# Expert entries: the hidden tile split into fp16 parts first and turned by a transposing DMA, with the down product one entry later

## The reference

```python
x = x + xattn(layernorm(x), ctx_512, Wq, Wkv_expand, Wout)      # 8 x 512 tokens of 512, 16 heads, 64 keys
x = x + ffn(layernorm(x), router_w, wg, wu, wd, sg_*, su_*, sd_*)

def ffn(x):
    logits = x @ router_w.T
    scores, top_idx = top_k(logits, 2)                          # 2 of 8 experts for each token
    comb = zeros((T, 8)).at[arange(T)[:, None], top_idx].set(scores)
    h = silu(x @ wg[e]) * (x @ wu[e])                           # 256 wide, for each expert e
    y = h @ wd[e]
    return sum_e(y * comb[:, e]) + shared_expert(x)
```

## Time and profile before

| | |
|---|---|
| median of 3 executions | 908.63 us |
| the profiled execution's own time | 908.0 us |
| its span, first to last instruction | 905.8 us |
| PE busy | 814.4 us (90%) |
| weight loads | 549.3 us (61%) |
| DVE busy | 664.5 us (73%) |
| ACT busy | 406.4 us (45%) |
| POOL busy | 379.6 us (42%) |
| DMA queue of SP (q1) | 29.5% of 16 engines |
| DMA queue of POOL (q0) | 22.3% of 16 engines |

### The profile page before, as it was taken

How to read it: one execution, slowest core, us unless ns; L and a number is a source line. 1 busy time by engine, 2 the same in 40 slices (tenths; PEclk the granted TensorE clock), 3 DMA queues, 4 the chain that set the end, 5 groups by cost and what they waited for, 6 DMA issues and landing times.

```text
span 905.8 us, 22405 instructions
## 1 busy us (share of the span) xinstructions
PE 814.4 (90%) x7626; PEld 549.3 (61%) x7626; DVE 664.5 (73%) x1352; ACT 406.4 (45%) x737; POOL 379.6 (42%) x486
## 2 busy tenths in 40 slices
PE   5378999888888888898999789999999999999995
PEld 2267777767666777676787668555555555555552
DVE  4999999999999999986467888555555555555552
ACT  3355757575657666666432223333333333333331
POOL 1114545454545364544300001355555655555553
PEclk9789999999999999999999999999999999999998
DMA  8233453536363634244675456375656666666661
GB/s 313 94 87 139 123 173 114 198 94 205 105 205 105 183 116 125 84 117 147 215 230 176 141 162 202 96 122 104 117 107 117 116 108 115 112 111 117 112 111 16
DMA packets 64136, 123.08 MB, mean 136 GB/s; under 512 B 15744, under 2 KB 16768, under 8 KB 62656
## 3 DMA queue, kind: packets, MB, share of 16 engines
q1 hardware_dynamic: 48160, 86.43, 29.5%
q0 software_dynamic: 15904, 35.70, 22.3%
HBM read 71.61 MB, written 52.31 MB: 137 GB/s over the span
## 4 chain that ended last, share of the span: by engine, by line
PE 49%; DVE 29%; issue 11%; POOL 5%; ACT 3%; DMA 1%; DVEq 1%; POOLq 1%; SPq 0%; ACTq 0%
PE psum L1202 34%; PE psum L1250 8%; PE psum L1193 6%; DVE stats L863 4%; DVE head_max L939 3%; DVE probsT L788 3%; DVE xy L949 2%; POOL kv_store L526 2%; DVE xn1T L788 2%; DVE emag L875 1%; DVE qT L788 1%; POOL rstd L507 1%; DVE probs L935 1%; DVE attnT L914 1%; DVE emax L890 1%
## 5 line engine op out<-in xcount | busy, mean ns | idle before, releaser
L616 POOL DMA_INDIRECT x_in<-normed_tokens,tabs x71 | 70.4, 991 | 228.8 <-DVE y_w L1150 126.5
L626 POOL DMA_INDIRECT out<-w_q,tabs x71 | 112.5, 1585 | 43.5 <-issue 18.1
L1168 DVE SCALAR_TENSOR_TENSOR hid<-psum,tabs,silu_g 128x256 f32<-128x256 f32 x71 | 34.3, 484 | 111.8 <-ACT silu_g L750 111.8
L1202 PE MATMUL psum<-exp_all,hidT 128*128 x426 | 103.5, 379 | 1.0 <-DVE hidT L1136 1.0
L1250 PE MATMUL psum<-xn1T,w_q 128*128 128x128 f16 x1536 | 93.5, 222 | 7.1 <-DVE xn1T L788 7.0
L750 ACT ACTIVATE silu_g<-psum,tabs 128x256 f32<-128x256 f32 x71 | 33.7, 474 | 146.1 <-PE psum L1202 146.1
L1202 PE MATMUL psum<-exp_all,probsT 128*128 x420 | 96.4, 379 | 0.0
L1250 PEld LDWEIGHTS psum<-xn1T,w_q 128*128 128x128 f16 x1536 | 88.5, 99 | 8.1 <-DVE xn1T L788 7.8
L1202 PE MATMUL psum<-w_o,attnT 128*128 128x512 f16 x384 | 89.0, 382 | 0.0
L505 POOL TENSOR_SCALAR rstd<-moments 128x1 f32<-128x1 f32 x64 | 14.2, 223 | 171.1 <-DVE moments L866 167.3
L518 POOL TENSOR_TENSOR exp_all<-piece,exp_all 128x512 f32 (+1 forms) x48 | 56.0, 1166 | 45.5 <-ACT piece L646 45.5
(11 more groups left out here) (197 smaller groups left out, 1704.8 us busy)
## 6 DMA issues: line engine op xcount, KB each, us to landing
x_in<-x SPq DMA_DIRECT2D x64, 256.0 KB, 3.0
exp_all<-experts SPq DMA_DIRECT2D x8, 1536.0 KB, 7.2
out<-xy SPq DMA_DIRECT2D x32, 256.0 KB, 2.0
normed_tokens<-xn SPq DMA_DIRECT2D x32, 256.0 KB, 2.1
normed_turned<-xn2T SPq DMA_DIRECT2D x32, 256.0 KB, 2.0
w_q<-out SPq DMA_DIRECT2D x32, 256.0 KB, 3.0
out<-w_q SPq DMA_DIRECT2D x32, 256.0 KB, 2.2
probsT<-normed_turned SPq DMA_DIRECT2D x16, 256.0 KB, 4.1
```

Source lines behind the costliest of these rows:

```text
L616: pool.indirect_dma_start(x_in[:, t % 4, :], None, xn_dram, bass.IndirectOffsetOnAxis(gather_at[:, t:t + 1], 0)).then_inc(gathered[t % 4], 16)
L626: pool.indirect_dma_start(out, bass.IndirectOffsetOnAxis(add_at[:, t:t + 1], 0), y[:, t % Y_RING, :], None, bounds_check=TOKENS - 1, oob_i ...
L1202: last = pe.matmul(dst, lhsT(a, c), rhs(z, c), start=(c == 0 and a == z == 0), stop=(c == n - 1 and a == 1))
```

## The change

For the ranked entries, `hid` is no longer turned on PE. ACT copies it to fp16 as it stands (high part), DVE makes the low part as it stands (`hid_parts`, two slots), and SP issues one transposing DMA from the 128 x 512 fp16 parts into one of now four slots of `hidT`. The down product of ranked tile k stands in entry k + 3 in place of k + 2, and `y` with it. `y_w` and the expert numbers get four slots. There is one entry more at the end. The shared expert's entries stay as they were. On SP the transposing DMA of t stands ahead of the turn of the add of t - 1, in one queue.

```diff
-        hidT = sb("hidT", [P, 2, 2, CI, P], F16)
+        hidT = sb("hidT", [P, 4, 2, CI, P], F16)
+        hid_parts = sb("hid_parts", [P, 2, 2, I], F16)
...
-        y_w = sb("y_w", [P, 2, 1])
+        y_w = sb("y_w", [P, 4, 1])
...
-            for n in range(2 * LAG - 3, ENTRIES + 2):
+            for n in range(2 * LAG - 3, ENTRIES + 3):
                 entry(n)
...
+        def down_at(n):
+
+            k = n - 2 if n - 2 < T else n - 3
+            return k if 0 <= k < ENTRIES and not (k == T - 1 and n == T + 2) else None
...
             sp.wait_ge(adds_ready, 1)
-            for t in range(3, SLOTS):
+            def turn_hid(t):
+                sp.wait_ge(parts_ready, t + 1)
+                wait(sp, down_mm, T + t - 3)
+                sp.dma_start_transpose(hidT[:, t % 4, :, :, :].rearrange("p v c q -> p (v c) q"),
+                                       hid_parts[:, t % 2, :, :].rearrange("p v i -> p (v i)")
+                                       ).then_inc(hid_turned[t % 4], 16)
+
+            def pass_turn(t):
                 before_t = sp.value_load(adds_before[0:1, t - 1:t], min_val=16, max_val=16 * SLOTS)
                 sp.wait_ge(y_added[(t - 1) % 2], before_t)
                 sp.sem_inc(add_turn, 1)
+
+            for t in range(SLOTS + 1):
+                if t < SLOTS:
+                    turn_hid(t)
+                if t >= 4:
+                    pass_turn(t - 1)
...
                 if tk is not None:
-                    act.wait_ge(hidT_mm, tk + 1)
-                    wait(act, down_mm, k - 1)
-                    copy(flat(hidT[:, k % 2, 0, :, :]), psum[:, HT_BANK[k % 2], 0:I], 1.0, hidT_hi)
+                    act.wait_ge(hid_ready, k + 1)
+                    if tk >= 2:
+                        act.wait_ge(hid_turned[(tk - 2) % 4], 16 * ((tk - 2) // 4 + 1))
+                    copy(hid_parts[:, tk % 2, 0, :], hid[:, :], 1.0, parts_hi)
...
                 if tk is not None:
-                    dve.wait_ge(hidT_hi, k + 1)
-                    dve.tensor_tensor(flat(hidT[:, k % 2, 1, :, :]), psum[:, HT_BANK[k % 2], 0:I],
-                                      flat(hidT[:, k % 2, 0, :, :]), ALU.subtract).then_inc(hidT_ready, 1)
+                    dve.wait_ge(parts_hi, tk + 1)
+                    dve.tensor_tensor(hid_parts[:, tk % 2, 1, :], hid[:, :], hid_parts[:, tk % 2, 0, :], ALU.subtract
+                                      ).then_inc(parts_ready, 1)
...
-                        wait(dve, hidT_mm, tm)
+                        wait(dve, parts_ready, tm)
...
-                if tk is not None:
-                    pe.wait_ge(hid_ready, k + 1)
-                    wait(pe, hidT_ready, k - 1)
-                    transposes(bank(HT_BANK[k % 2]), hid, CI, hidT_mm)
...
-                if elive(k):
-                    pe.wait_ge(hidT_ready, k + 1)
+                k = down_at(n)
+                if k is not None:
+                    tk = ranked(k)
+                    if tk is None:
+                        pe.wait_ge(hidT_ready, k + 1)
+                    else:
+                        pe.wait_ge(hid_turned[tk % 4], 16 * (tk // 4 + 1))
                     wait(pe, y_ready, k - 1)
```

More of the change, by code:

```diff
@@ L276, in xattn_moe @@
         y_stored = [sem(f"y_stored{i}") for i in range(Y_RING)]
-        xg_mm, xgT_hi, xgT_ready, gate_mm, up_mm, silu_ready, hid_ready, hidT_mm, hidT_hi, hidT_ready = [
-            sem(n) for n in ("xg_mm", "xgT_hi", "xgT_ready", "gate_mm", "up_mm", "silu_ready", "hid_ready", "hidT_mm",
-                             "hidT_hi", "hidT_ready")]
+        xg_mm, xgT_hi, xgT_ready, gate_mm, up_mm, silu_ready, hid_ready, hidT_hi, hidT_ready = [
+            sem(n) for n in ("xg_mm", "xgT_hi", "xgT_ready", "gate_mm", "up_mm", "silu_ready", "hid_ready", "hidT_hi", "hidT_ready")]
+        parts_hi, parts_ready, hid_turned = sem("parts_hi"), sem("parts_ready"), [sem(f"hid_turned{i}") for i in range(4)]
         down_mm, y_w_made, y_w_ready, y_ready = [sem(n) for n in (
@@ L1148, in entry @@
                     dve.wait_ge(y_w_made, tm + 1)
-                    dve.wait_ge(y_ready, m - 1)
-                    dve.tensor_reduce(y_w[:, tm % 2, :], y_w_terms[:, :], AX.X, ALU.add).then_inc(y_w_ready, 1)
+                    dve.wait_ge(y_ready, m - 3)
+                    dve.tensor_reduce(y_w[:, tm % 4, :], y_w_terms[:, :], AX.X, ALU.add).then_inc(y_w_ready, 1)
                 if elive(m):
@@ L1166, in entry @@
                             dve.wait_ge(hidT_ready, m)
-                        wait(dve, hidT_mm, tm)
+                        wait(dve, parts_ready, tm)
                         dve.scalar_tensor_tensor(hid[:, :], psum[:, GU_BANK[m % 2], I:2 * I], up_scale_at[:, tm:tm + 1],
                                                  silu_g[:, :], ALU.mult, ALU.mult).then_inc(hid_ready, 1)
-                if elive(k):
+                kd = down_at(n)
+                if kd is not None:
+                    k, tk = kd, ranked(kd)
                     dve.wait_ge(down_mm, k + 1)
@@ L1180, in entry @@
                             dve.wait_ge(y_added[tk % 2], 16 * (tk // 2 - 1))
-                        dve.tensor_scalar(y[:, k % Y_RING, :], bank(DOWN_BANK[k % 2]), y_w[:, tk % 2, :], None, ALU.mult
+                        dve.tensor_scalar(y[:, k % Y_RING, :], bank(DOWN_BANK[k % 2]), y_w[:, tk % 4, :], None, ALU.mult
                                           ).then_inc(y_ready, 1)
@@ L1340, in hot @@
                 last.then_inc(hot_used, 1)
-            expert_now = [None, None]
+            expert_now = [None] * 4
             def expert_at(t):
@@ L1376, in entry @@
                         pe.wait_ge(xgT_ready, tm + 1)
-                        e = expert_now[tm % 2]
+                        e = expert_now[tm % 4]
                         product(bank(GU_BANK[m % 2]), chunks(xgT[m % 4]),
                                 lambda v, c: expert_part(e, v, c * 2 * I, 2 * I), C, up_mm)
-                if elive(k):
-                    pe.wait_ge(hidT_ready, k + 1)
+                k = down_at(n)
[5 more added lines that the diff above has]
+                        pe.wait_ge(hid_turned[tk % 4], 16 * (tk // 4 + 1))
                     wait(pe, y_ready, k - 1)
@@ L1387, in entry @@
                     else:
-                        e = expert_now[tk % 2]
-                        product(bank(DOWN_BANK[k % 2]), chunks(hidT[:, k % 2]),
+                        e = expert_now[tk % 4]
+                        product(bank(DOWN_BANK[k % 2]), chunks(hidT[:, tk % 4]),
                                 lambda v, c: expert_part(e, v, GU + c * H, H), CI, down_mm)
@@ L1394, in entry @@
                         pe.wait_ge(piece_split, E * PIECES)
-                    expert_now[t % 2] = expert_at(t)
+                    expert_now[t % 4] = expert_at(t)
             over_tiles(pe, step, entry)
```

## The result

The changed kernel takes **893.98 us** (median of 4 runs, 892.88 to 895.16) against 908.49 us for the kernel before in the same session (4 runs, 908.34 to 910.14). The ratio is 0.9836, with a 95% interval of 0.9819 to 0.9854: 1.6% less, 14.5 us. The forecast was 891.8 us, the range 887 to 905.

What follows compares the result with a forecast made beforehand. PE's instructions were taken as the bound: 908.0 - 20.3 (70 entries at 0.29 us) + 3.5 at the end = 891.2 us, and 0.6 from that execution to the median gives 891.8 us; range 887 to 905 us.

Steps and rivals of the forecast that it cites:

- The period: Ranked entries: without two PE transposes, each falls from 4.609 to 4.32 us, 20.3 us over 70 entries.
- Parts, ACT and DVE: ACT's copy (0.51 us) and DVE's low part (0.42 us) per entry cost nothing, hidden behind PE.
- The slack of 5.9 us: Per entry, the transposing DMA has 712.71 - 706.8 = 5.9 us from its wait to its landing.
- The 3.4 us: Landing time taken for the transposing DMA, what a gather needs under the same load; leaves 2.5 us of slack.
- The cheap bound of 2.0: Lowest landing time for the transposing DMA, from a plain 256 KB store out of SBUF on the same queue.
- part of the gain is given back: Rival: the transposing DMA lands after 5.9 to 6.8 us, period (7.05 + L) / 3, 904 us; chance 0.08.
- Two signs that the prediction named for being wrong: In the loop: gathers landing late, and PE waiting at the rows' transposes.
- The DMA engines: Per entry, a transposing DMA is 64 packets, 0.36 us of each engine, raising their share to 0.78.
- The rival by which turns of 2.85 us hold every engine: Transposing DMAs set a period of 5.85 us, 87 us lost, near 1000 us; within slower, chance 0.13.
- The estimate for four blocks: Transposing DMA: four blocks one after the other take 5.2 us, longer than an entry, giving about 956 us.
- The end: Last down product but one to last scaling goes from 4.27 to 7.75 us, costing 3.5 us, uncovered.
- moved, not new: PE's work in the extra entry is the down product that was moved; no gain was counted.

Runs made afterwards that it cites:

- e2: The kernel before, with only the down product one entry later and four slots of hidT, PE still transposing: 910.62 us, ratio 1.001.
- e1: The changed kernel with its down product put back to entry k + 2, the transposing DMA kept: 998.23 us, ratio 1.0964.
- b0: The changed kernel run again, unaltered, as base for the kernels timed beside it: 894.6 us, ratio 0.9823 to the kernel before.
- g0: The changed kernel run again, unaltered, in the third session: 892.24 us, ratio 0.9814 to the kernel before.
- b1: The changed kernel with the last ranked tile alone transposed on PE, as in the kernel before: 891.57 us, ratio 0.9788.
- e3: The changed kernel with a second transposing DMA of the same parts per ranked entry, into unread space: 902.5 us, ratio 0.9887 without its last run.
- e4: The changed kernel without the transposing DMA, the down product waiting for the parts and reading old hidT slots: 890.57 us, ratio 0.9766.

## Why the prediction was right

*The period.* The entry without the two transposes, 4.32 us by the earlier trace rows, is what the changed kernel runs: 4.322. Of the gain, 20.3 us were forecast from it and 20.1 measured. e2 shows that it comes from PE's work, and not from a tie undone; e1 that this order of work has it only with the later place.

*Parts, ACT and DVE.* As worked out: both free, the parts ready 1.3 us after the next entry begins (1.4 forecast), and the add issued 0.83 us behind `y` (0.8 forecast, 3.1 before).

*The slack of 5.9 us and the landing.* This was the step on which everything hung, and it held in kind. The 3.4 us were good as a median (3.3 measured, 3.5 in b0, 3.4 in g0), though a gather beside it, from which the figure was taken, now needs 4.7 us: the right value came in part by luck. The cheap bound of 2.0 is near what a turn takes with next to nothing beside it (2.4 at the end). The slack was read rightly: turns over 5.9 us stall PE, shorter ones don't. What the working lacked is the tail: landings reach 6.9 us in the first profile, and 1 to 6 of some 70 are over 5.9 in the profiles of this kernel and of b1. They, and gathers that come late under the same load, cost 1.1 to 6.2 us per execution there, where the prediction had none in its likeliest case and a fixed lateness in the rival "part of the gain is given back". That rival's formula takes a late landing in every entry; what came is a rare one, paid once each. Two signs that the prediction named for being wrong came in part: gathers land late (4.7 us), and in b0 PE waits for one at the rows' transposes, once.

*The DMA engines.* The price was mis-sized: 0.36 us of each engine per turn predicted, 0.97 measured, 540 packets and not 64. It moved no period of the median entry, for the share isn't the limit that the prediction took it for: e3 ran at 1.12 with a median period of 4.322. The rival by which turns of 2.85 us hold every engine is excluded by the same row. Where the true limit of these engines lies, no run shows.

*The estimate for four blocks.* Four blocks land in 2.4 us at the end, 0.6 us a block at most, where the Trainium skill's page "VectorE: DVE Perf Modes", section The three transpose paths, has 1309 ns for one block. So the estimate of 5.2 us, and the 956 us with it, doesn't hold here. The runs show landings of blocks in one transfer, not of a single block.

*The end.* 7.72 us measured, 7.75 forecast, but that is luck: two errors cancel. The last turn landed in 2.4 us and not 3.4, with no gather and hardly any add beside it; the last product took 2.53 us and not 1.47. The windows of the changed kernel around that wait, clock in the last column but two:

```profile
879.00:881.40 2.40, 0.04 (x1) 0.00 (x0) 0.75 (x1) 0.00 (x0) 1.55 (x1) 1.00 0.31 59
881.40:884.00 2.60, 2.53 (x6) 0.76 (x6) 0.00 (x0) 0.00 (x0) 1.55 (x1) 0.56 0.03 1
```

PE was idle for 2.4 us, then ran at a granted clock of 0.56, about the lower of its two levels. In b0 the same product after the same wait ran at full speed (1.47 us), because there the clock fell only after it. So the end costs 2.4 to 3.5 us, some 0.9 of it from the shift alone (e2).

*Not counted:* 1.3 us from the one entry that has no down product, which the prediction put aside as "moved, not new". It is moved into the end, whose cost was already summed, so it counts as a gain (a row of e2 shows the condition: nothing may wait for `hid` there).

*Left open:* why the first stage ends up to 5 us apart between executions, when the clock falls at the end, and whether it is the add or the gather behind it that makes a landing long.

## What to carry to other kernels

Work can be taken off the engine that is the bound by giving it to a DMA, if the consumer is first moved so far that the slack exceeds the landing; one entry more or less decided here between 1.6% faster and 10% slower. Price that slack against the longest landing under the load of the loop, not against the median or an idle queue, and expect the rest as single stalls. Look at what is issued just ahead of the long ones: here each had an add less than 3 us before it. At the end of a pipeline, where nothing covers a landing, keep the short path for the last tile, and look first at what issues the last stores.

## What the runs showed of the hardware

- A transposing DMA of 128 x 512 fp16 inside SBUF: 2.4 us with next to nothing beside it, 3.3 us median and up to 6.9 beside gathers and adds (8.0 in b1), 1.19 us of SP's queue to issue, 540 packets.
- Of 423 such landings in six profiles 17 took over 5.9 us, all with an indirect add issued less than 3 us ahead.
- The DMA share of the profile can exceed 1 (1.12 in e3) while the loop keeps its pace.
- Gathers of an unchanged size went from 3.4 to 4.3 us by the later place alone (e2; e4 the same).
- After a wait of 2.4 us PE's next six matmuls took 2.53, 2.09 and 1.47 us in three executions of one kernel, at a granted clock of 0.56, 0.66 and 1.00.
